# A graph layer on one core: the one-hot matrices built a pair ahead, and the gather ring released by TensorE

## The chip, the cores and the metric

The kernel runs on one core of a Trainium2 chip. Its time is the device time of one execution in microseconds (us); the timed runs give a median, and one further execution was recorded by the hardware profiler. Engines are named as the profile names them: PE is the matrix engine (PEld its weight loads), DVE the vector engine, ACT the scalar engine, POOL the general engine that also issues gathers, SP the engine that issues plain DMAs.

## What is computed

A graph of 12,500 nodes with 256 features and 212,500 directed edges (100,000 pairs both ways, and one loop per node), sorted by destination. Three parts are added up:

```python
def gcn_conv(x, W, b, src, dst, num_nodes):
    h = x @ W
    ...                                   # loops added once more, degrees, norm = dinv[s] * dinv[d]
    msg = h[s] * norm[:, None]
    out = jax.ops.segment_sum(msg, d, num_segments=num_nodes)
    return out + b

xn = _layernorm(x)
x = x + gnn(xn) + mix(xn)                 # gnn: gcn_conv(256->128), relu, gcn_conv(128->256)
x = x + ffn(_layernorm(x))                # ffn on the half of the nodes with the largest routing weight
```

`mix` is a linear attention: a softmax of the keys over all nodes, its product with the values, a normalization, and the product with the queries. `ffn` is two products (256 to 1024 to 256) with a GELU between, scaled by the node's routing weight. The segment sum over the edges, done once per layer of the GNN, is what this change is about.

## The kernel before, in words

Nodes are held in 98 tiles of 128 (`TILES`). Edges are cut into chunks of 128, sixteen chunks make a pair of batches (`PAIR`), and there are 104 pairs (`PAIRS`), 8 chunks to each batch, called a half (`HALF`). For each layer and each pair:

1. POOL (`gather_layer`, L493) issues 16 indirect gathers; each fetches 128 rows of 128 numbers from a table in DRAM (`table`) into the ring, which holds two pairs, that is four quarters of 8 chunks. Ahead of each half it waits until that quarter of the ring is free.
2. DVE builds for each half the one-hot matrices `S`: for each chunk a 128x128 matrix that says which edge goes to which node of a window of 128 nodes. It first takes each edge's distance to the start of the window (`drel`, L1162, 128x8), and then compares it with a ramp held in a PSUM bank (`ramp2`), four chunks at a time (L1171, 128x512, two per half).
3. PE (`visit`, L745) multiplies the 8 matrices with the 8 gathered chunks into PSUM bank `visit_sum[h]`, one bank for each half: 8 products, which the trace shows as 16 records (the operands are float32).
4. DVE (`add`, L1182) adds the bank into the accumulator `acc`, which lies in SBUF for all tiles; a window straddles two tiles, so there are two masked operations of 128x128.
5. DVE then releases the quarter: L1192 and L1193 in `other_visits` raise the semaphore `ring_half_free` on which POOL waits in front of the half that is two pairs later.

Where a batch reaches over more than one window of 128 nodes, further visits follow in a loop (`other_visits`).

The engines are otherwise filled with other work, written out by hand into the pairs. In layer 1, pairs 0 to 97 also take one tile each of the mixer: DVE `mix_1` (L1215 to L1221, the running maximum of the keys), ACT (L584 to L590, the exponentials), PE (L774 transposes, L780 products), DVE `mix_3` (L1226 to L1231), and PE and ACT for the next keys (L760, L767, L579, L582). DVE `finish_layer_1` (L1202, L1204) finishes a tile of the accumulator once no later edge reaches it, and SP writes it to the table of layer 2. In layer 2, pairs take the tiles' feed-forward: DVE `ff_1` (L1317, L1320), PE (L850 to L859), DVE `ff_norm` (L1326 to L1332), PE L866, ACT L612, PE L873 (first product), ACT L616 (GELU), PE L883 (second product), DVE `ff_3` (L1349, L1351) and `ff_route` (L1338 to L1343). Which tile is due in which pair stands in a control table of four words a pair (`ctl`), made during setup, that DVE and PE read into registers at the start of each pair (L329).

Order on DVE within a pair, before: read of the control words, next indices, both builds (in layer 2 with `ff_route` and `ff_1` between them), add of half 0 and its release, mixer or feed-forward work, add of half 1 and its release.

## Time and profile before

| | us |
|---|---|
| timed runs, median of 3 | 5739.89 (5737.28 to 5745.67) |
| profiled execution | 5720.82 |
| its span, first to last instruction | 5719.0 |
| setup, until POOL's first gather of layer 1 | 230.5 |
| gathers of layer 1 | 2509.4 (230.5 to 2739.9) |
| pause between the layers | 21.7 |
| gathers of layer 2 | 2806.7 (2761.6 to 5568.3) |
| last adds, feed-forward tail, selection, output | 150.7 |
| busy in the span: PE, POOL, DVE, ACT | 2936.6, 3250.5, 1904.3, 1214.9 |

An engine's busy time leaves out its register, branch and semaphore instructions. A bracket at the end of a timeline row gives the idle time of the engine before that row and what ended it: "DVEq L1193" is the release instruction in DVE's queue, "issue" that nothing the profile shows was waited for, and "remote" that the releaser could not be matched with an instruction of this core that had just ended.

### The profile page before, as it was taken

To read this page: it belongs to the slowest core of one execution; us is meant where nothing else is said; L and a number is where in the kernel's file an instruction comes from. 1 tells how busy PE (TensorE), PEld (TensorE's weight loads), DVE (VectorE), ACT (ScalarE), POOL (GpSimd) and SP (SyncE) were. 2 spreads that over 40 slices of the span, in tenths; PEclk is the share of its full clock that TensorE was granted. 3 is DMA by queue.
4 is the path that set the end of the run, shared out by engine and by line. 5 is a ranking of instruction groups with operands and counts; after the bars stand their busy time and mean duration, and the time that the engine had idled before them with its cause. 6 is when DMAs were issued, how large, how long until landed. Compare 5 with 4: busy or idle time off the path is not lost.

```text
span 5719.0 us, 69449 instructions
## 1 busy us (share of the span) xinstructions
PE 2936.6 (51%) x16356; PEld 2523.6 (44%) x16357; DVE 1904.3 (33%) x5571; ACT 1214.9 (21%) x2622; POOL 3250.5 (57%) x3443
## 2 busy tenths in 40 slices
PE   6544334444433343443266566656656666666663
PEld 5433333333333333333255455555555555555552
DVE  8433333333333233332133233323333332333336
ACT  3311111111111111110022222222223222322221
POOL 4566666666666666666555555555555555555550
PEclk8766666666666666666587778777778787787776
DMA  3211111111111111111211111111111111111115
GB/s 108 70 45 46 46 46 47 46 46 46 45 46 46 45 46 46 46 46 46 55 45 44 42 43 45 43 42 42 45 45 42 44 45 41 43 44 45 42 42 183
DMA packets 191338, 288.38 MB, mean 50 GB/s; under 512 B 59596, under 2 KB 137588, under 8 KB 191094
## 3 DMA queue, kind: packets, MB, share of 16 engines
q0 software_dynamic: 106496, 218.32, 13.4%
q1 hardware_dynamic: 83572, 68.55, 3.8%
q10 hardware_dynamic: 1232, 1.05, 0.1%
q8 instruction: 19, 0.31, 0.0%
q14 instruction: 19, 0.16, 0.0%
HBM read 249.19 MB, written 38.49 MB: 50 GB/s over the span
## 4 chain that ended last, share of the span: by engine, by line
another core or an unknown queue 34%; issue 19%; PE 16%; DVE 14%; DVEq 11%; ACT 5%; POOL 0%; DMA 0%; ACTq 0%; SPq 0%; POOLq 0%
PE bank L883 6%; PE bank L745 3%; DVEq L329 3%; PE bank L873 3%; DVE arena L1171 2%; DVE acc L1182 2%; ACT arena L616 1%; DVE drel L1162 1%; DVEq L1240 1%; DVEq L1229 1%; DVEq L1162 1%; DVE arena L1027 1%; PE bank L859 1%; DVE arena L1231 1%
## 5 line engine op out<-in xcount | busy, mean ns | idle before, releaser
L493 POOL DMA_INDIRECT arena<-table,idx_now x3328 | 3148.3, 946 | 2202.5 <-DVEq L1193 1110.8
L745 PE MATMUL bank<-arena 128*128 128x128 f32 x6656 | 1108.9, 328 | 625.3 <-issue 397.3
L745 PEld LDWEIGHTS bank<-arena 128*128 128x128 f32 x6656 | 1050.3, 242 | 667.4 <-issue 654.2
L1182 DVE SCALAR_TENSOR_TENSOR acc<-bank,from_base,acc 128x128 f32 x416 | 145.0, 349 | 1601.4 <-remote 1551.7
L774 PE MATMUL bank<-ident,arena 128*128 128x128 f32 x196 | 67.3, 447 | 1145.7 <-ACT arena L586 1130.1
L873 PE MATMUL bank<-arena 128*128 128x128 f32 x3136 | 509.5, 338 | 253.9 <-ACT arena L612 163.1
L1171 DVE TENSOR_TENSOR arena<-bank,drel 128x512 f32<-128x512 f32 x832 | 536.0, 686 | 244.7 <-issue 190.6
L873 PEld LDWEIGHTS bank<-arena 128*128 128x128 f32 x3136 | 490.8, 251 | 277.6 <-ACT arena L612 176.7
L883 PE MATMUL bank<-arena 128*128 128x256 f32 x1568 | 498.9, 479 | 159.6 <-ACT arena L616 109.3
L774 PEld LDWEIGHTS bank<-ident,arena 128*128 128x128 f32 x196 | 28.2, 203 | 1164.5 <-ACT arena L586 1148.6
L883 PEld LDWEIGHTS bank<-arena 128*128 128x128 f32 x1568 | 375.6, 248 | 261.3 <-ACT arena L616 130.4
L616 ACT ACTIVATE arena<-bank,fb1col 128x128 f32<-128x128 f32 x784 | 218.4, 374 | 1121.4 <-remote 990.5
L584 ACT ACTIVATE sm<-sm 128x2 f32<-128x2 f32 x98 | 19.9, 203 | 1653.0 <-DVEq L1222 1644.4
L780 PE MATMUL bank<-arena 128*128 128x256 f32 x392 | 203.2, 674 | 61.1 <-ACT arena L590 60.0
L1196 DVE CAST idx_now<-src_idx (+1 forms) x208 | 38.2, 184 | 510.3 <-issue 510.3
L1162 DVE TENSOR_SCALAR drel<-dst_of,tile_base,iota_n 128x8 f32 (+1 forms) x416 | 133.4, 321 | 210.4 <-issue 178.0
L760 PE MATMUL bank<-ident,arena 128*128 128x128 f32 x196 | 67.6, 449 | 218.1 <-issue 216.0
L579 ACT ACT_TABLE_LOAD x97 | 124.5, 1283 | 232.2 <-issue 165.5
L780 PEld LDWEIGHTS bank<-arena 128*128 128x128 f32 x392 | 115.0, 323 | 117.8 <-ACT arena L590 98.4
L608 ACT ACTIVATE arena<-bank 128x384 f32<-128x384 f32 x98 | 48.0, 490 | 523.5 <-PE bank L852 387.3
L760 PEld LDWEIGHTS bank<-ident,arena 128*128 128x128 f32 x196 | 28.5, 204 | 288.1 <-issue 285.3
L1182 DVE SCALAR_TENSOR_TENSOR acc<-bank,below_base,acc 128x128 f32 x416 | 142.2, 342 | 0.0
(237 smaller groups left out, 3079.6 us busy)
## 6 DMA issues: line engine op xcount, KB each, us to landing
arena<-table,idx_now POOLq DMA_INDIRECT x3328
base_rows<-arena SPq DMA_DIRECT2D x98, 128.0 KB
xs<-in_x_dram SPq DMA_DIRECT2D x6, 1792.0 KB, 16.4
acc<-base_rows SPq DMA_DIRECT2D x9, 896.0 KB, 9.8
out_dram<-acc SPq DMA_DIRECT2D x8, 896.0 KB, 7.7
table<-acc SPq DMA_DIRECT2D x7, 896.0 KB, 4.8
table<-acc SPq DMA_DIRECT2D x98, 64.0 KB
arena<-base_rows SPq DMA_DIRECT2D x5, 896.0 KB, 11.8
```

The source lines that it names most:

```text
L329: _, words = nc.values_load_multi_w_load_instructions(ctl[0:1, ds(g, 1), 0:4].rearrange("p a c -> p (a c)"), engines=[engine_type], min_val=0,
L493: pool.indirect_dma_start(ring[:, quarter * HALF + k, :], None, table[layer], bass.IndirectOffsetOnAxis(ap=idx_now[:, i, c:c + 1], axis=0) ...
L579: act.activation(xn, xs[:, ds(t, 1), :].rearrange("p a d -> p (a d)"), ACT.Identity, bias=nmr[:, ds(t, 1)], scale=rstd[:, ds(t, 1)]).then_ ...
L616: last = act.activation(H[:, k, :], pH[half][:, (k % 4) * P:(k % 4 + 1) * P], ACT.Gelu_apprx_tanh, bias=fb1col[:, k:k + 1])
L745: last = nc.tensor.matmul(visit_sum[h][:, 0:F], S[:, h, k, :], ring[:, quarter * HALF + k, :], start=(k == 0), stop=(k == HALF - 1))
L760: last = nc.tensor.transpose(pT[:, k * P:(k + 1) * P], xn[:, k * P:(k + 1) * P], ident[:, :])
L780: last = nc.tensor.matmul(pG[:, k * D:(k + 1) * D], En[:, k, :], xn, start=True, stop=True)
L873: last = nc.tensor.matmul(pH[h // 4][:, (h % 4) * P:(h % 4 + 1) * P], fw1[:, k, h * P:(h + 1) * P], T3[:, k, :], start=(k == 0), stop=(k = ...
L883: last = nc.tensor.matmul(pY[:, 0:D], H[:, h, :], fw2[:, h, :], start=(h == 0), stop=(h == KH - 1))
L1162: dve.tensor_scalar(drel[:, h, :], dst_of[:, ds(g * PAIR + h * HALF, HALF)], tile_base[:, ds(t, 1)], iota_n[:, ds(turn, 1)], ALU.subtract, ...
L1171: dve.tensor_tensor(S[:, h, 4 * q:4 * q + 4, :], bc(ramp2[:, ds(turn, P)].rearrange("p (a n) -> p a n", a=1), [P, 4, P]), bc(drel[:, h, 4 ...
L1182: last = dve.scalar_tensor_tensor(a, visit_sum[h][:, 0:F], mask[:, ds(turn, 1)], a, ALU.mult, ALU.add)
```

## The change

Four things are changed.

- The one-hot matrices of a half are built in one operation of 128x1024 that subtracts the window's start and compares at once. The starts stand in a new tile `base_col` (one column a half), which setup makes with one more PE product. `drel`, `tile_base` and their semaphores go.
- They are built a pair ahead: behind the add of half h of pair g, DVE builds half h of pair g+1. The first pair's are built ahead of each layer's loop (`first_builds`), and the last pair is written out behind the loops.
- POOL waits for PE's own signal `visit_summed` of the half two pairs earlier (it starts at 2, so that the first two pairs find the ring free). DVE no longer releases anything. PE no longer waits for the add, since DVE's build comes behind it, and it waits once per half for `S` and not twice.
- Batches that reach over several windows get a loop of their own at the start of a pair (`extra_visits`), behind which `S` is zeroed and the normal visit follows. The control words are packed anew: DVE reads three and PE two.

```diff
-            dve.sem_inc(s_free[layer], 4)
+            dve.sem_inc(s_sum[layer][h], 2)            # for each h
...
-                            pool.wait_ge(s_free[layer], gg * (2 * SETS) + (2 * i + h + 1))
+                            pool.wait_ge(s_sum[layer][h], gg * SETS + (i + 1))
...
-            def visit(layer, batch, gg, quarter, i):
-                pe.wait_ge(s_gath[layer][quarter], gg * (16 * HALF) + 16 * HALF)
-                pe.wait_ge(s_fl[layer][h], v + 1)
+            def visit(layer, gg1, g1, quarter):
+                h = quarter % 2
+                pe.wait_ge(s_gath[layer][quarter], gg1)
+                pe.wait_ge(s_S[layer][h], g1)
+                sum_half(h, quarter).then_inc(s_sum[layer][h], 1)
...
-            def build(layer, batch, g, h, i):
-                dve.tensor_scalar(drel[:, h, :], dst_of[:, ds(g * PAIR + h * HALF, HALF)], tile_base[:, ds(t, 1)],
-                                  iota_n[:, ds(turn, 1)], ALU.subtract, ALU.add).then_inc(s_drel[layer][h], 1)
-                dve.wait_ge(s_drel[layer][h], v + 1)
-                for q in range(2):
...
-                    dve.tensor_tensor(S[:, h, 4 * q:4 * q + 4, :],
-                                      bc(ramp2[:, ds(turn, P)].rearrange("p (a n) -> p a n", a=1), [P, 4, P]),
-                                      bc(drel[:, h, 4 * q:4 * q + 4].rearrange("p (c a) -> p c a", a=1), [P, 4, P]),
-                                      ALU.is_equal).then_inc(s_S[layer][h][q], 1)
+            def build(g, h, turn, base):
+                return dve.scalar_tensor_tensor(
+                    S[:, h], bc(dst_of[:, ds(g * PAIR + h * HALF, HALF)].rearrange("p (c a) -> p c a", a=1), [P, HALF, P]),
+                    base, bc(ramp2[:, ds(turn, P)].rearrange("p (a n) -> p a n", a=1), [P, HALF, P]),
+                    ALU.subtract, ALU.is_equal)
+            def build_main(layer, g, h, turn):
+                build(g, h, turn, base_col[:, ds(g * 2 + h, 1)]).then_inc(s_S[layer][h], 1)
...
+            def add_main(layer, h, place, g3):
+                dve.wait_ge(s_sum[layer][h], g3)
+                add(h, *place).then_inc(s_fl[layer][h], 1)
...
-                next_indices(0, g)
-                build(0, b0, g, 0, 0)
-                build(0, b1, g, 1, 0)
+                dve.wait_ge(s_fl[0][1], g)
+                next_indices(0, g)
+                extra_visits(0, g, at_places, extra)
                 with dve.If(f0 > 0):
                     finish_layer_1(t0)
                 if before is not None:
                     mix_3(before)
-                add(0, b0, 0, 0)
-                other_visits(0, b0, g, 0)
+                add_main(0, 0, at_places[0], g3)
+                if not last:
+                    build_main(0, g1, 0, turns[0])
                 if n is not None:
                     mix_1(g, n)
-                add(0, b1, 1, 0)
-                other_visits(0, b1, g, 1)
+                dve.wait_ge(s_fl[0][0], g1)
+                add_main(0, 1, at_places[1], g3)
+                if not last:
+                    build_main(0, g1, 1, turns[1])
...
                 next_indices(1, g)
-                build(1, b0, g, 0, 0)
+                extra_visits(1, g, at_places, extra)
                 with dve.If(f1 > 0):
                     ff_route(t1, Chain(Chain.PER - 2))
                 with dve.If(f0 > 0):
                     ff_1(t0, ch)
-                build(1, b1, g, 1, 0)
-                add(1, b0, 0, 0)
-                other_visits(1, b0, g, 0)
+                add_main(1, 0, at_places[0], g3)
+                if not last:
+                    build_main(1, g1, 0, turns[0])
                 with dve.If(f1 > 0):
                     ff_3(t1)
                 with dve.If(f0 > 0):
                     ff_norm(t0, ch)
-                add(1, b1, 1, 0)
-                other_visits(1, b1, g, 1)
+                dve.wait_ge(s_fl[1][0], g1)
+                add_main(1, 1, at_places[1], g3)
+                if not last:
+                    build_main(1, g1, 1, turns[1])
```

The order on POOL in layer 2's loop, before. One row is one instruction, `x7` seven like the one above it, and a bracket names the semaphores that a row waits for (`ring_half_free1` is raised by DVE behind the add, `visit_summed1_0` by PE at the end of a visit of half 0):

```order
L488 REGISTER_ALU [waits indices_ready1]
L493 DMA arena<-table,idx_now 128x128 [waits ring_half_free1]
L493 DMA arena<-table,idx_now 128x128 x7
L488 REGISTER_ALU
L493 DMA arena<-table,idx_now 128x128 [waits ring_half_free1]
```

And now:

```order
L482 REGISTER_ALU
L491 DMA arena<-table,idx_now 128x128 [waits indices_ready1,visit_summed1_0]
L491 DMA arena<-table,idx_now 128x128 x7
L491 DMA arena<-table,idx_now 128x128 [waits visit_summed1_1]
L491 DMA arena<-table,idx_now 128x128 x7
```

The sixteen gathers stand as they stood; what they wait for has moved from DVE to PE.

The order on DVE in layer 1's loop, from the end of `mix_3` to the start of `mix_1`, before. Ahead of these rows both builds of the same pair have been done; `visit_summed0_0` is PE's signal, and the If of `other_visits` and the release (L1192) follow the two adds:

```order
L1231 SCALAR_TENSOR_TENSOR arena<-arena,sm,bank5 128x256
L1182 ISA [waits visit_summed0_0]
L1182 SCALAR_TENSOR_TENSOR acc<-bank0,from_base,acc 128x128
L1182 ISA
L1182 SCALAR_TENSOR_TENSOR acc<-bank0,below_base,acc 128x128
L1187 REGISTER_ALU
L1187 COMPARE_AND_BRANCH
...
L1192 ISA
L1215 TENSOR_REDUCE sm<-bank3 128x2 [waits visits_added0_0,mix_keys_ready]
```

And now, up to the second build of the next pair:

```order
L1179 SCALAR_TENSOR_TENSOR acc<-bank0,from_base,acc 128x128
L1179 ISA
L1179 SCALAR_TENSOR_TENSOR acc<-bank0,below_base,acc 128x128
L1168 REGISTER_ALU x2
L1168 ISA
L1168 SCALAR_TENSOR_TENSOR arena<-dst_of,base_col,bank7 128x1024
L1234 TENSOR_REDUCE sm<-bank3 128x2 [waits mix_keys_ready]
...
L1179 SCALAR_TENSOR_TENSOR acc<-bank1,below_base,acc 128x128
L1168 REGISTER_ALU x2
L1168 ISA
L1168 SCALAR_TENSOR_TENSOR arena<-dst_of,base_col,bank7 128x1024
```

Between the add and `mix_1` the release is gone, and the first build of the next pair has come in.

## Rows read from the trace of the kernel before

**Rows 1.** Windows of both layers: length, then PE, PEld, DVE, ACT, POOL busy; PEclk.

```profile
230.50:2739.90 2509.40, 1000.10 (x4892) 845.47 (x4892) 757.98 (x2324) 351.62 (x888) 1571.57 (x1664) 0.64 0.16 46
2761.60:5568.30 2806.70, 1722.59 (x8863) 1491.93 (x8864) 867.16 (x2453) 741.07 (x1415) 1576.69 (x1664) 0.78 0.15 44
```

**Rows 2.** Waits of POOL, layer 1, 430 to 2650 us.

```profile
engine line waited for: us in total, times, longest us
POOL arena L493 <- issue: 419.4, 1376, 0.3
POOL arena L493 <- DVEq L1193: 415.2, 92, 6.5
```

**Rows 3.** The same of layer 2, 2860 to 5460 us.

```profile
POOL arena L493 <- DVEq L1193: 621.8, 111, 9.5
POOL arena L493 <- issue: 525.2, 1424, 8.5
```

**Rows 4.** Timeline, layer 1: start, duration (us), engine, operation, idle time before.

```profile
1509.70 0.94 POOL L493 DMA_INDIRECT arena<-table,idx_now  x1 [4.54 <-DVEq L1193]
...
1516.26 1.29 DVE L1171 TENSOR_TENSOR arena<-bank,drel 128x512 f32<-128x512 f32 x2
...
1517.13 3.67 PE L745 MATMUL bank<-arena 128*128 128x128 f32 x16
...
1517.50 0.35 DVE L1202 SCALAR_TENSOR_TENSOR acc<-acc,dinv,b1row 128x128 f32 x1
...
1518.44 0.94 POOL L493 DMA_INDIRECT arena<-table,idx_now  x1 [0.30 <-issue]
...
1528.43 0.94 POOL L493 DMA_INDIRECT arena<-table,idx_now  x1 [0.30 <-issue]
1532.43 0.35 DVE L1182 SCALAR_TENSOR_TENSOR acc<-bank,from_base,acc 128x128 f32 x1 [12.62 <-remote]
1532.70 0.34 DVE L1182 SCALAR_TENSOR_TENSOR acc<-bank,below_base,acc 128x128 f32 x1
...
1533.90 0.94 POOL L493 DMA_INDIRECT arena<-table,idx_now  x1 [4.53 <-DVEq L1193]
```

**Rows 5.** Timeline, end of layer 1, where no gather runs.

```profile
2748.00 6.28 PE L745 MATMUL bank<-arena 128*128 128x128 f32 x32 [16.69 <-DVE arena L1171]
...
2751.93 0.35 DVE L1182 SCALAR_TENSOR_TENSOR acc<-bank,from_base,acc 128x128 f32 x1 [1.87 <-PE bank L745]
```

**Rows 6.** Timeline, start of layer 2, behind forty gathers in a row.

```profile
2810.28 0.94 POOL L493 DMA_INDIRECT arena<-table,idx_now  x1 [0.30 <-issue]
2817.86 0.35 DVE L1182 SCALAR_TENSOR_TENSOR acc<-bank,from_base,acc 128x128 f32 x1 [33.02 <-remote]
...
2819.62 0.94 POOL L493 DMA_INDIRECT arena<-table,idx_now  x1 [8.40 <-issue]
```

**Rows 7.** Timeline, one pair of layer 2.

```profile
3625.03 0.94 POOL L493 DMA_INDIRECT arena<-table,idx_now  x1 [1.14 <-issue]
3625.56 0.38 ACT L612 ACTIVATE arena<-bank 128x256 f32<-128x256 f32 x1 [5.81 <-remote]
...
3636.87 1.61 PE L745 MATMUL bank<-arena 128*128 128x128 f32 x8 [1.83 <-issue]
...
3640.48 0.34 DVE L1182 SCALAR_TENSOR_TENSOR acc<-bank,from_base,acc 128x128 f32 x1
...
3641.95 0.94 POOL L493 DMA_INDIRECT arena<-table,idx_now  x1 [7.24 <-DVEq L1193]
```

**Rows 8.** Groups by line, layer 2: busy us, mean ns, idle before and releasers.

```profile
L745 PE MATMUL bank<-arena 128*128 128x128 f32 x3060 | 481.6, 306 | 416.6 <-issue 330.3 <-DVE arena L1171 85.3
```

**Rows 9.** Page part 5 and groups of layer 1: operations nearest to a build.

```profile
L1171 DVE TENSOR_TENSOR arena<-bank,drel 128x512 f32<-128x512 f32 x832 | 536.0, 686 | 244.7 <-issue 190.6
...
L1162 DVE TENSOR_SCALAR drel<-dst_of,tile_base,iota_n 128x8 f32 (+1 forms) x416 | 133.4, 321 | 210.4 <-issue 178.0
...
L1231 DVE SCALAR_TENSOR_TENSOR arena<-arena,sm,bank 128x256 f32<-128x256 f32 x184 | 80.2, 477 | 30.5 <-issue 25.2 <-PE bank L780 2.7
```

More of the change, by code:

```diff
@@ new lines, in control_words, with places, next_turns @@
+                ctl[0:1, ds(g, 1), first:first + n].rearrange("p a c -> p (a c)"), engines=[engine_type], min_val=0,
+                max_val=(1 << 31) - 1, skip_runtime_bounds_check_because=own_table)
+            return words
+        def places(eng, word):
+            return [(within(eng, (word >> (16 * h + 7)) & (P - 1), 0, TILES - 1),
+                     within(eng, (word >> (16 * h)) & (P - 1), 0, P - 1)) for h in range(2)]
+        def next_turns(eng, word):
+            return [within(eng, (word >> (16 + 8 * h)) & (P - 1), 0, P - 1) for h in range(2)]
@@ L990, in _ @@
             dve.memset(ones_row, 1.0)
+            dve.tensor_scalar(rrow[:, 12, :], lo_r, float(1 - P), None, ALU.add)
             link(dve.memset(zeros_b, 0.0))
@@ L1182, in add @@
                     last = dve.scalar_tensor_tensor(a, visit_sum[h][:, 0:F], mask[:, ds(turn, 1)], a, ALU.mult, ALU.add)
-                last.then_inc(s_fl[layer][h], 1)
-            def other_visits(layer, batch, g, h):
-                _, _, windows, first = batch
-                with dve.If(windows > 1):
-                    with dve.Fori(1, windows) as i:
-                        build(layer, batch, g, h, i)
-                        add(layer, batch, h, i)
-                dve.wait_ge(s_fl[layer][h], first + windows + 1)
-                dve.sem_inc(s_free[layer], 1)
+                return last
@@ new lines, in add_main, with extra_visits @@
+            def add_main(layer, h, place, g3):
+                dve.wait_ge(s_sum[layer][h], g3)
+                add(h, *place).then_inc(s_fl[layer][h], 1)
+            def extra_visits(layer, g, at_places, word):
+                with dve.If(word > 0):
+                    for h, (begin, windows) in enumerate(extra_steps(dve, mybir.EngineType.DVE, g, word)):
+                        tile, turn = at_places[h]
+                        base = sm[:, 61:62]
+                        dve.tensor_copy(base, base_col[:, ds(g * 2 + h, 1)]).then_inc(s_xb[layer], 1)
+                        dve.wait_ge(s_xb[layer], begin + 1)
+                        dve.sem_inc(s_passed, 1)
+                        with dve.Fori(0, windows) as i:
+                            build(g, h, turn, base).then_inc(s_xS[layer], 1)
+                            dve.wait_ge(s_xsum[layer], begin + i + 1)
+                            here = nc.s_assert_within(
+                                tile + i, 0, TILES - 1,
+                                skip_runtime_bounds_check_because="a window begins at or below a node of the graph")
+                            add(h, here, turn).then_inc(s_xfl[layer], 1)
+                            dve.wait_ge(s_xfl[layer], begin + i + 1)
+                            dve.tensor_scalar(base, base, float(P), None, ALU.add).then_inc(s_xb[layer], 1)
+                            dve.wait_ge(s_xb[layer], begin + i + 2)
+                            dve.sem_inc(s_passed, 1)
+                        dve.memset(S[:, h], 0.0).then_inc(s_xS[layer], 1)
+                        dve.sem_inc(s_xfl[layer], 1)
@@ L1195, in next_indices, with first_builds @@
+            def first_builds(layer):
+                now, = control_words(mybir.EngineType.DVE, 0, 0, 1)
+                for h, (_, turn) in enumerate(places(dve, now)):
+                    build_main(layer, 0, h, turn)
             def next_indices(layer, g):
@@ L1355, in ff_route_and_3, with pair_of_layer_2 @@
                 ff_3(t)
-            with dve.Fori(0, PAIRS) as g:
-                (b0, b1), (t0, f0), (t1, f1) = read_control(dve, mybir.EngineType.DVE, g)
+            def pair_of_layer_2(g, last=False):
+                g1, g3 = (g + 1, g + 3) if isinstance(g, int) else (dve.snap(g + 1), dve.snap(g + 3))
+                now, flags, extra = control_words(mybir.EngineType.DVE, g, 0, 3)
+                at_places, turns = places(dve, now), next_turns(dve, flags)
+                (t0, f0), (t1, f1) = (stage(dve, flags, k) for k in range(2))
                 ch = Chain()
+                if not isinstance(g, int) or g > 0:
+                    dve.wait_ge(s_fl[1][1], g)
                 next_indices(1, g)
-                build(1, b0, g, 0, 0)
+                extra_visits(1, g, at_places, extra)
                 with dve.If(f1 > 0):
```

210 lines of the change are left out of this document (107 added, 103 removed).

## The prediction

> **What bounds the kernel now.** I read the windows first. Both layers have the same 1,664 gathers and nearly the same POOL time (1571.57 and 1576.69 us), yet take 2509.40 and 2806.70 us [rows 1]. No engine is busy all the time in either: PE is busy 1000 of 2509 us and 1723 of 2807, DVE 758 and 867. So a chain of waits sets the time, and POOL, whose gathers start everything, is the place to read it. Per pair that is 24.1 us in layer 1 (2509.40 / 104) and 27.0 in layer 2 (2806.70 / 104).
>
> The waits of POOL come second. In layer 1 there is the regular pause of 0.30 us between two gathers (419.4 us, 1376 times), and a wait for the DVE instruction that frees a half of the ring: 92 times, 415.2 us, so 4.51 us each, once a pair [rows 2]. In layer 2 the waits sum to 621.8 + 525.2 = 1147.0 us, of which 0.30 x 1535 = 461 us are regular; about 686 us over 96 pairs, 7.1 us a pair, are stalls [rows 3]. The gathers themselves cost 16 x (0.94 + 0.30) = 19.9 us a pair: the floor under both layers.
>
> The timeline, third, shows what a stall is made of. In layer 1 POOL gathers from 1509.70 to 1529.37 (16 gathers, last start 1528.43). PE's visit 0 begins at 1517.13 and is over at 1520.80, visit 1 follows. DVE has nothing else to do from then on, and waits 12.62 us, until 1532.43, to add the visit's sum; POOL goes on at 1533.90 [rows 4]. So the sum was there 11.6 us before DVE learned of it, and DVE learned of it 3.06 us after the last gather. Where no gather runs, the same add follows PE by 1.87 us [rows 5]; behind forty gathers it waits 33.02 us, until 6.6 us after the last one (2810.28 + 0.94 to 2817.86), and POOL pauses 8.40 us [rows 6]. I read this so: what PE signals late in a long stretch of gathers is delivered only when the stretch has ended. The wait is for a signal and not for arithmetic. The Trainium skill (Perfetto Trace Analysis, section Per-instruction lifecycle) says that a matmul's reported end is an estimate and that the propagation of a semaphore is in no reported time. By that alone the 11.6 us could be a late end of PE and would stay whoever waits; but the 1.87 us of the undisturbed add holds both hidden parts, so the sum is the same by either.
>
> **The release of the ring (POOL waits for PE itself).** Before: signal of PE, two masked adds on DVE, two branch instructions, the release, POOL. Now: signal of PE, POOL. The adds take from 1532.43 to 1533.04, and POOL starts 0.86 us behind them [rows 4]. Lower bound of the gain: the adds alone, 0.61 us. Upper: POOL starts when DVE now wakes, 1.47 us. POOL needs a time of its own to answer a signal, as it needs now within the 0.86; I take 0.85 us, nearer the lower bound. The 3.06 us of late signal stay, because now it is POOL that waits for that signal. Layer 1: 102 stalls (two pairs are free at the start) x 0.85 = 87 us (62 to 150); its pause would go from 4.5 to about 3.7 us. The second half's signal has come by then, and its 0.6 us are hidden under the first half's gathers.
>
> In layer 2 DVE has work in front of the add: at 3636.87 PE runs the last eight records of a visit until 3638.48, but DVE adds at 3640.48, behind ff_1 and the second build, and POOL starts at 3641.95 [rows 7]. With the answer time of the undisturbed case (1.87 us [rows 5]) POOL could start at 3640.35, 1.6 us earlier; with 0.9 us behind PE's last record, 2.6. The second half has a pause of 1.14 us (start 3625.03), of which the add's 0.6 can go [rows 7]. Together 2.2 to 3.2 us a pair on POOL's side. I do not believe all of it: PE goes through the pair in one order, visit, ff_1, visit, ff_hidden, and its chain through ACT has delayed signals too (the copy at 3625.56 waited 5.81 us) [rows 7]. If that chain sets the period, an earlier gather only waits longer to be used. Bounds: 0.8 us (what layer 1 gains, the chain absorbs the rest) and 3.4 us (the stalls of 7.1 shrink to layer 1's new 3.7). I take 1.6 us, between 0.8 and the 2.2 that POOL's side offers at its cautious end: 102 x 1.6 = 163 us (82 to 347).
>
> **The build in one operation, a pair ahead.** Four tensor_tensor of 0.686 us and two small ones for the differences, 0.32 us each (3.4 us a pair), become two operations of 128x1024. That form is not in the trace. The nearest rows are 0.477 us for 128x256 and 0.686 for 128x512 [rows 9]; carried on by the same slope (0.209 us per 256) that is 1.10, with the slope of 1 ns an element 1.20, and two builds as they stand cost 1.37. I take 1.2, so DVE is busy 1.0 us less a pair, at most 1.2. On the path this is worth nothing in layer 1: DVE is idle for 12.62 us a pair [rows 4]. It adds one thing there: the first build now stands between the add and mix_1, so mix_1 and PE's transposes, which stand ahead of visit 0, start up to 1.2 us later. Visit 0 ended 8.6 us before the gathers did (1520.80 against 1529.37) [rows 4], so the gathers hide it. If that cover were gone it would cost 102 x 1.2 = 122 us.
> In layer 2 it takes the second build (1.3 us) from in front of the add, which is counted above, and PE no longer waits for a build (85.3 us in all, 41 times) [rows 8]. Part of that is on the chain PE to ACT to PE; it is inside my 1.6.
>
> **Port contention.** Gathers keep their 0.30 us pauses beside a build (1516.26) and beside an operation with two inputs in SBUF (1517.50 against the gather at 1518.44) [rows 4], so a long DVE operation costs POOL nothing. The Trainium skill (SBUF — State Buffer, section SBUF: two separate sides) says that GpSimd cannot write descriptors while VectorE holds the shared port pair for a whole instruction, in a two-port mode. No run here shows such a block. By the rule the new operation, int16 from SBUF against PSUM, would have to be in such a mode to hurt; that is the first slower rival below.
>
> **Control words, setup, boundary.** DVE reads three words and PE two instead of four with checks; both reads are off the path in layer 1, and I count nothing. Setup grows by some ten small linked operations; at the 0.32 us of the small L1162 [rows 9] that is +3 us. At the end of layer 1 PE's last two visits wait for their builds (16.69 us idle, then the product at 2748.00) [rows 5]; built a pair ahead, they need not. The two builds and two small operations of a half are 1.7 us, the read ahead of them about as much again: -4 us, bounds -1.7 and -6. The loop for wider batches does not run with these inputs: the 3060 records of L745 in some 96 pairs are 32 a pair, 16 for each half, no visit more [rows 8].
>
> **Sum.** -87 - 163 + 3 - 4 = -251 us of the profiled execution's 5720.82 (span 5719.0). The median of the timed runs, 5739.89, stands 19 us above it, and the difference is taken from that: 5739.89 - 251 = 5489 us, 4.4% less.
>
> **Rivals.**
> 1. The feed-forward chain sets layer 2, and only the signal path counts: 0 to 0.8 us a pair in layer 2, 0.6 in layer 1. 5740 - 61 - 41 = 5638 us. For it: PE is busiest there and ACT's waits are long. Against it: PE works 1723 of 2807 us, not all of them.
> 2. The stalls of layer 2 fall to layer 1's: 3.4 us a pair. 5740 - 87 - 347 = 5306 us. For it: both layers have the same gathers. Against it: the slow issue on PE late in the stretch of gathers (records 1.83 us apart) [rows 7].
> 3. The signals are no longer late, since POOL itself now waits for them or since the gathers fall into shorter stretches: the floor, 208 x 19.9 = 4150 us in place of 5316, less a fill: about 4600 to 4800 us. Nothing in the trace speaks for it; the lateness is there at the end of every stretch.
> 4. Slower: restarting POOL straight at PE's signal begins the next stretch of gathers before DVE, ACT and PE have taken their own signals from the one before. In layer 2, work that now slips through in the open 7 us (visit, add, GELU, the next product) then falls into the stretch, where a signal costs up to 12.6 us [rows 4] or 33 [rows 6]. It decides when visit 0's end is pushed behind the last gather by more than today's 3.8 us (3638.48 against 3641.95 - 7.24 = 3634.71) [rows 7] plus the gain. With the 8.40 us pause of rows 6 at each pair in place of 7.1, +1.3 us, and the loss of my gain, layer 2 is 130 us longer and layer 1 87 shorter: 5783 us.
> 5. Slower: a build blocks POOL for its length: 2 x 1.2 us x 208 = +500 us, less 251: about 5990. Chance 2 in 100, since no operation beside the gathers does so now.
>
> **Chances.** Forecast, with its own range of 5380 to 5600: 0.50. Rival 1: 0.20. Rival 2: 0.14. Rival 3: 0.03. Rival 4 and its weaker forms around no change: 0.11. Rival 5: 0.02. A measurement tells 0.2%, 11.5 us, from no change. Faster 0.86, same 0.03, slower 0.11. The range of 8 in 10 takes in rivals 1 and 2: 5260 to 5660 us.
>
> **What the new profile would show.** Right: POOL's stall has PE as its releaser, and is 3.5 to 3.9 us once a pair in layer 1; DVE's add in layer 1 still waits about 11 us for a late signal; one operation of 128x1024 of about 1.2 us, 416 of them; layer 2 near 25.4 us a pair. Wrong: a stall of layer 1 that stays at 4.5 us or grows (the signal comes later when POOL is the one that waits), visit 0 ending behind the last gather in layer 1, pauses between two gathers of more than 0.30 us beside a build, or a period of layer 2 at or above 27 us with PE's records spread further apart.

## The result and the profile after

The changed kernel takes 5439.59 us (median of 4 runs, 5438.04 to 5449.98), the kernel before 5738.59 (5703.95 to 5745.67). The ratio is 0.949 (95% interval 0.946 to 0.952), a gain of 299 us where 251 were forecast. The profiled execution took 5439.44 us, its span is 5437.7.

By stage, read from POOL's first and last gather of each layer in the two traces:

| us | before | after | difference | forecast |
|---|---|---|---|---|
| setup, to the first gather | 230.5 | 241.4 | +10.9 | +3 |
| gathers of layer 1 | 2509.4 | 2470.2 | -39.2 | -87 |
| between the layers | 21.7 | 15.8 | -5.9 | -4 |
| gathers of layer 2 | 2806.7 | 2564.7 | -242.0 | -163 |
| tail | 150.7 | 145.6 | -5.1 | 0 |

The rows add up to -281, the difference of the two profiled executions; the profiled one of before ran 18 us under its median.

The page after, part 5:

```profile
L491 POOL DMA_INDIRECT arena<-table,idx_now x3328 | 3144.1, 945 | 1919.3 <-issue 1338.9
...
L1168 DVE SCALAR_TENSOR_TENSOR arena<-dst_of,base_col,bank 128x1024 f32 (+1 forms) x416 | 532.3, 1280 | 19.9 <-issue 18.0
```

And POOL's row on the page before:

```profile
L493 POOL DMA_INDIRECT arena<-table,idx_now x3328 | 3148.3, 946 | 2202.5 <-DVEq L1193 1110.8
```

The build is there as one operation, 416 times, at 1.28 us (the estimate was 1.2, from [rows 9]). POOL's idle time has fallen from 2202.5 to 1919.3 us.

The windows of both layers (length, then PE, PEld, DVE, ACT and POOL busy, PE's clock), against [rows 1]:

```profile
241.40:2711.60 2470.20, 996.58 (x4908) 836.47 (x4908) 695.86 (x1913) 351.70 (x888) 1570.05 (x1664) 0.64 0.18 47
2727.50:5292.10 2564.60, 1634.87 (x8877) 1407.57 (x8877) 810.42 (x2044) 743.23 (x1419) 1573.97 (x1664) 0.81 0.18 48
```

POOL's busy time is the same as before to within 3 us; all of the gain is idle time of POOL. PE is busy 88 us less in layer 2, at a higher clock (0.81 against 0.78).

POOL's waits in mid layer 1 and mid layer 2 (us in total, times, longest), against [rows 2, 3]:

```profile
POOL arena L491 <- issue: 619.5, 1387, 4.7
POOL arena L491 <- remote: 172.2, 46, 3.8
POOL arena L491 <- PE bank L735: 17.7, 58, 0.3
POOL arena L491 <- DVE idx_now L1215: 3.6, 2, 3.3
...
POOL arena L491 <- issue: 564.7, 1393, 5.9
POOL arena L491 <- PE bank L735: 178.7, 45, 6.0
POOL arena L491 <- remote: 165.0, 68, 2.7
```

The release by DVE is gone; the one row of DVE is the wait for the next indices. In layer 1 "issue" now hides half of the stalls: its longest is 4.7 us, where an ordinary pause is 0.30. Stalls and pauses together were 835 us in the same window before, and are 813 now; in layer 2 they were 1147 in 2600 us, and are 910 in 2340.

A stretch of layer 1 (start, duration, engine, line, idle time before), against [rows 4]. The first row is the end of a visit, whose sum DVE adds at 1512.87:

```profile
1499.82 1.39 PE L735 MATMUL bank<-arena 128*128 128x128 f32 x11
...
1506.32 0.17 DVE L1240 COPY sm<-sm 128x2 f32<-128x2 f32 x1
1506.57 0.20 ACT L582 ACTIVATE sm<-sm 128x2 f32<-128x2 f32 x1 [11.87 <-DVEq L1241]
...
1507.28 0.20 ACT L584 ACTIVATION_READ_ACCUMULATOR arena<-bank,sm 128x1 f32 x1
1507.53 0.69 PE L774 MATMUL bank<-ident,arena 128*128 128x128 f32 x2 [6.32 <-ACT arena L584]
1508.45 0.94 POOL L491 DMA_INDIRECT arena<-table,idx_now  x1 [0.30 <-issue]
1512.36 0.38 ACT L588 ACTIVATE arena<-bank 128x256 f32<-128x256 f32 x1 [4.89 <-remote]
...
1512.87 0.35 DVE L1179 SCALAR_TENSOR_TENSOR acc<-bank,from_base,acc 128x128 f32 x1 [6.39 <-remote]
...
1513.95 0.94 POOL L491 DMA_INDIRECT arena<-table,idx_now  x1 [4.55 <-issue]
...
1517.48 3.75 PE L735 MATMUL bank<-arena 128*128 128x128 f32 x16
...
1521.70 0.35 DVE L1179 SCALAR_TENSOR_TENSOR acc<-bank,from_base,acc 128x128 f32 x1 [4.34 <-issue]
...
1532.67 0.94 POOL L491 DMA_INDIRECT arena<-table,idx_now  x1 [0.30 <-issue]
1536.58 0.38 ACT L588 ACTIVATE arena<-bank 128x256 f32<-128x256 f32 x1 [7.68 <-remote]
...
1537.09 0.35 DVE L1179 SCALAR_TENSOR_TENSOR acc<-bank,from_base,acc 128x128 f32 x1 [9.17 <-remote]
1537.31 0.94 POOL L491 DMA_INDIRECT arena<-table,idx_now  x1 [3.69 <-remote]
```

The stall is still there: the last gather starts at 1508.45, ends at 1509.39, and only at 1512.36 do ACT and then DVE (1512.87) go on, behind work of PE whose records end at 1508.22 and 1501.21. In the same stretch of gathers signals from DVE to ACT (1506.49 to 1506.57) and from ACT to PE (1507.48 to 1507.53) come at once: it is PE's signals that are late. The recorded semaphore updates of layer 1 say the same, in both kernels: those of DVE, ACT and POOL stand 0.01 us behind the end of their instruction, those of PE a median of 9.7 us behind it before and 3.4 us now, at most 12.1 and 13.7. The end of a PE record is modelled, so the traces leave open whether PE itself ends late or its signal is held.

What is new is where the stall stands. Before, POOL paused ahead of the first half of nearly every pair of layer 1 (3 of its 103 long pauses stood ahead of a second half). Now the first half's signal comes through in the middle of the stretch (PE's visit ends at 1521.2, DVE adds at 1521.70), and the pause is ahead of the second half. And the pauses alternate: POOL goes on 1.59 us behind ACT's wake at 1513.95, but 0.73 us behind it at 1537.31 (from 1536.58). The longer one is always ahead of the second half of an odd pair.

In layer 2, against [rows 7]:

```profile
3610.33 0.35 DVE L1179 SCALAR_TENSOR_TENSOR acc<-bank,from_base,acc 128x128 f32 x1 [8.42 <-remote]
...
3610.69 0.94 POOL L491 DMA_INDIRECT arena<-table,idx_now  x1 [2.53 <-remote]
...
3646.18 0.94 POOL L491 DMA_INDIRECT arena<-table,idx_now  x1 [5.85 <-issue]
```

POOL starts 0.36 us behind DVE's first add; before it started 1.47 us behind it (3640.48 to 3641.95). The third row is the long pause of the next pair, ahead of its second half: layer 2 still has stalls ahead of both halves.

### The profile page after: what moved, and what is told of

The parts are those of the page before. It is cut to its first block, busy times and chain, and to the rows that moved or that the text cites. A ratio compares the mean times of both kernels' runs of the same rounds, so it can differ in the third digit from the quotient of the medians.

```text
span 5437.7 us, 61242 instructions
## 1 busy us (share of the span) xinstructions
PE 2844.7 (52%) x16358; PEld 2429.4 (45%) x16359; DVE 1781.9 (33%) x4751; ACT 1216.2 (22%) x2622; POOL 3246.4 (60%) x3442
## 4 chain that ended last, share of the span: by engine, by line
another core or an unknown queue 29%; issue 28%; PE 22%; ACT 8%; DVE 7%; DVEq 3%; POOL 2%; DMA 0%; ACTq 0%; SPq 0%; POOLq 0%
PE bank L735 5%; PE bank L883 5%; PE bank L873 4%; PE bank L780 3%; DVE arena L1168 1%; ACT arena L614 1%; POOL arena L491 1%; ACT arena L584 1%; ACT L577 1%; ACT L608 1%; PE bank L760 1%; PE bank L859 1%; PE bank L663 1%; ACT arena L588 1%
## 5 line engine op out<-in xcount | busy, mean ns | idle before, releaser
L491 POOL DMA_INDIRECT arena<-table,idx_now x3328 | 3144.1, 945 | 1919.3 <-issue 1338.9
L735 PE MATMUL bank<-arena 128*128 128x128 f32 x6656 | 1082.6, 321 | 427.8 <-issue 321.5
L735 PEld LDWEIGHTS bank<-arena 128*128 128x128 f32 x6656 | 1016.2, 235 | 479.5 <-issue 404.3
L873 PE MATMUL bank<-arena 128*128 128x128 f32 x3136 | 484.6, 327 | 228.8 <-ACT arena L610 174.1
L873 PEld LDWEIGHTS bank<-arena 128*128 128x128 f32 x3136 | 466.0, 240 | 252.9 <-ACT arena L610 189.7
L883 PE MATMUL bank<-arena 128*128 128x256 f32 x1568 | 475.7, 461 | 171.9 <-ACT arena L614 115.8
L1168 DVE SCALAR_TENSOR_TENSOR arena<-dst_of,base_col,bank 128x1024 f32 (+1 forms) x416 | 532.3, 1280 | 19.9 <-issue 18.0
L780 PE MATMUL bank<-arena 128*128 128x256 f32 x392 | 203.3, 674 | 549.0 <-ACT arena L588 549.0
L883 PEld LDWEIGHTS bank<-arena 128*128 128x128 f32 x1568 | 353.2, 234 | 262.3 <-ACT arena L614 141.9
L780 PEld LDWEIGHTS bank<-arena 128*128 128x128 f32 x392 | 115.2, 324 | 604.9 <-ACT arena L588 587.3
L582 ACT ACTIVATE sm<-sm 128x2 f32<-128x2 f32 x98 | 19.9, 203 | 1141.3 <-issue 608.7
L1234 DVE TENSOR_REDUCE sm<-bank 128x2 f32<-128x256 f32 x98 | 41.5, 423 | 451.0 <-remote 360.8
L588 ACT ACTIVATE arena<-bank 128x256 f32<-128x256 f32 x98 | 37.5, 383 | 577.6 <-remote 577.6
```

The costliest lines, as they stand in the source:

```text
L491: pool.indirect_dma_start(ring[:, quarter * HALF + k, :], None, table[layer], bass.IndirectOffsetOnAxis(ap=idx_now[:, i, c:c + 1], axis=0) ...
L588: act.activation(En.rearrange("p k n -> p (k n)"), pE[:, 0:D], ACT.Copy).then_inc(s_mEe, 1)
L735: last = nc.tensor.matmul(visit_sum[h][:, 0:F], S[:, h, k, :], ring[:, quarter * HALF + k, :], start=(k == 0), stop=(k == HALF - 1))
L780: last = nc.tensor.matmul(pG[:, k * D:(k + 1) * D], En[:, k, :], xn, start=True, stop=True)
L873: last = nc.tensor.matmul(pH[h // 4][:, (h % 4) * P:(h % 4 + 1) * P], fw1[:, k, h * P:(h + 1) * P], T3[:, k, :], start=(k == 0), stop=(k = ...
L883: last = nc.tensor.matmul(pY[:, 0:D], H[:, h, :], fw2[:, h, :], start=(h == 0), stop=(h == KH - 1))
```

## The experiments

Theory A says that the signal's way from PE to POOL is the gain. Theory B says that building ahead is. Each set of kernels ran together with the kernel before, and each ratio is to that.

### First set: what part of the change gains

**Only the release moved** (`e1`, on the kernel before):

```diff
-                            pool.wait_ge(s_free[layer], gg * (2 * SETS) + (2 * i + h + 1))
+                            pool.wait_ge(s_sum[layer][h], gg * SETS + (i + 1))
...
-                dve.wait_ge(s_sum[layer][h], v + 1)
+                dve.wait_ge(s_sum[layer][h], v + 3)      # the count starts at 2
```

> The kernel before, with only POOL's wait moved from DVE's release to PE's signal; builds in three operations and in their old place. Theory A (the signal path is what gains): layer 1 loses 0.4 to 0.85 us a pair, layer 2 about 1.6, so 5738.6 - 40 to 87 - 163 = about 5490 to 5540 us. Theory B (the building a pair ahead is what gains in layer 2, since PE and the feed-forward chain set it): only layer 1 and a little of layer 2 gain, about 5650 us, and layer 2 stays above 26.5 us a pair.

Measured: 5432.70 us, ratio 0.947 (0.944 to 0.951): the whole gain of the change. Layer 1 takes 2425.3 us (-84), layer 2 2593.6 (-213). Two rows of its layer 1, the last gather ahead of a stall and the first behind it:

```profile
1515.88 0.94 POOL L493 DMA_INDIRECT arena<-table,idx_now  x1 [0.30 <-issue]
...
1520.50 0.94 POOL L493 DMA_INDIRECT arena<-table,idx_now  x1 [3.68 <-remote]
```

The pause is 3.68 us, against 4.53 before [rows 4]: 0.85 us less, as forecast. Theory A is right, B fell. The stall stays ahead of the first half here, as before.

**The builds back at their pair** (`e2`, on the changed kernel):

```diff
                 next_indices(0, g)
                 extra_visits(0, g, at_places, extra)
+                for h in range(2):
+                    build_main(0, g, h, at_places[h][1])
...
-                if not last:
-                    build_main(0, g1, 0, turns[0])
...
                     ff_1(t0, ch)
+                build_main(1, g, 1, at_places[1][1])
                 add_main(1, 0, at_places[0], g3)
```

> The changed kernel with both builds (one operation each) back at their place before: at the start of their own pair, in layer 2 one before the router step and one before the add. Theory A: POOL no longer hangs on DVE, so the place of the builds matters little: 5440 to 5480 us. Theory B: layer 2 goes back by one to two us a pair: 5550 to 5650 us.

Measured: 5446.96 us, ratio 0.950 (0.947 to 0.953), the same as the changed kernel within the intervals. Layers: 2479.3 and 2569.8 us, 9 and 5 us more than with the builds ahead. Building ahead is worth nothing that this measurement can tell, once POOL doesn't hang on DVE. The stall of layer 1 stands ahead of the second half as in the changed kernel, so it is not the place of the builds that moved it.

**The release back on DVE** (`e3`, on the changed kernel):

```diff
-                            pool.wait_ge(s_sum[layer][h], gg * SETS + (i + 1))
+                            pool.wait_ge(s_free[layer], gg * (2 * SETS) + (2 * i + h + 1))
...
                 add(h, *place).then_inc(s_fl[layer][h], 1)
+                dve.wait_ge(s_fl[layer][h], g3 - 2)
+                dve.sem_inc(s_free[layer], 1)
```

> The changed kernel, but POOL again waits for a release that DVE gives behind its add (and ahead of the next build). Theory A: 0.8 us a pair more in layer 1 (about 85 us) and 0.8 to 1.6 in layer 2 (80 to 160): 5600 to 5680 us. Theory B: half of it or less, since DVE now reaches its add without a build in front: 5480 to 5520 us.

Measured: 5673.11 us, ratio 0.990 (0.987 to 0.993). Layer 1 takes 2593.1 us, 84 more than before the change; layer 2 takes 2670.1, 137 less. From its layer 1:

```profile
1514.01 0.94 POOL L492 DMA_INDIRECT arena<-table,idx_now  x1 [0.30 <-issue]
...
1518.47 0.35 DVE L1181 SCALAR_TENSOR_TENSOR acc<-bank,from_base,acc 128x128 f32 x1 [9.76 <-remote]
...
1520.80 0.94 POOL L492 DMA_INDIRECT arena<-table,idx_now  x1 [5.84 <-issue]
```

POOL goes on 2.33 us behind the start of DVE's add (this is the half with the longer answer; before it was 1.47). Against the changed kernel, layer 1 takes 123 us more, where 85 were expected. So everything in the change but the release is worth 1%: it loses 84 us in layer 1, where the stall stands ahead of the second half here too, and gains 137 in layer 2. That the latter comes of the add no longer standing behind a build is read from the order on DVE, not tested by itself. With the release on PE the same thing is worth nothing, since POOL doesn't ask for the add: the two gains are not to be added up.

**mix_1 ahead of the build** (`e4`, on the changed kernel):

```diff
+                if n is not None:
+                    mix_1(g, n)
                 if not last:
                     build_main(0, g1, 0, turns[0])
-                if n is not None:
-                    mix_1(g, n)
```

> The changed kernel with the first build of the next pair behind mix_1 in layer 1, and not ahead of it. If the gathers hide mix_1 (as predicted), no change: 5430 to 5450 us. If the mixer's chain is late by the build's 1.28 us and sets when the second half's signal goes out, layer 1 gains up to 1.2 us a pair: 5320 to 5400 us.

Measured: 5442.32 us, ratio 0.949 (0.946 to 0.952); layer 1 2469.6 us against 2470.2. The build's 1.28 us in front of the mixer is hidden, as forecast. Here too the stall stands ahead of the second half. What moved it there is left among the rest of the change (control words, the order of waits on PE, the build in one operation), which no run takes apart.

### Second set: what makes the signals late, and a set in which none was

**Two gathers of eight** (`e6`), **the ring turned** (`e7`), **a pause behind each fourth gather in layer 1** (`e8`), **no loop for wide batches** (`e9`), all on the changed kernel:

```diff
-                            for k in range(HALF):                       # e6
+                            for k in range(2):
...
-                                    ring[:, quarter * HALF + k, :], None, table[layer],          # e7
+                                    ring[:, place_of[quarter] * HALF + k, :], None, table[layer],   # [3, 0, 1, 2]
...
                                 ).then_inc(s_gath[layer][quarter], 16)      # e8
+                                if k % 4 == 3 and layer in (0,):
+                                    idled[0] += 1
+                                    pool.memset(arena[:, 11400:11400 + 512], 0.0).then_inc(s_idle[layer], 1)
+                                    pool.wait_ge(s_idle[layer], gg * 16 + idled[0])
...
-                extra_visits(0, g, at_places, extra)      # e9, on DVE and PE, both layers
```

> The changed kernel with two gathers in each half and not eight; PE multiplies the eight matrices with these two chunks in turn (six of eight gathers are left out, all products stay). Theory A (PE's signals are held back by long stretches of gathers): a pair's gathers are over in 5 us, no signal is late, DVE's add follows PE by about 1.9 us, and a pair of layer 1 takes 12 to 16 us, one of layer 2 16 to 20. Theory C (PE's products end late by themselves, or their signal takes 9 to 12 us whatever POOL does): the add still waits 9 us or more behind PE's last record, and a pair of layer 1 stays above 20 us.

> The changed kernel with the ring's quarters laid to other addresses (first half of even pairs into the last quarter, the others one further down); order, semaphores and code stay. In the changed kernel POOL starts its first gather 0.77 us behind the end of a wait, but 1.62 us where the gather goes to the last quarter (second half of odd pairs). If that goes with the address, the second halves of odd pairs start 0.85 us earlier: about 45 us less in layer 1 (where nearly all pauses are ahead of second halves) and 0 to 20 in layer 2, 5375 to 5400 us. If it goes with the place in the code or the semaphore: no change, 5440 us.

> The changed kernel; in layer 1 POOL clears a spare 128x512 piece of SBUF behind every fourth gather and waits for the end of it (an idle DMA queue of about 1 us, four times a pair). Theory A with short memory (a stretch under 5 us delays no signal and a short pause ends it): DVE's adds follow PE in 2 us, the 4 us pause of a pair vanishes and four of about 1 us take its place: layer 1 within 1% of now, pause about 4 us in all, 5400 to 5480 us. Theory A with long memory (a pause of 1 us doesn't let the signals through): the stall stays and the pauses come on top, 3 to 4 us a pair, 5750 to 5850 us.

> The changed kernel without the loop for batches over several windows (code and branch are left out; no batch of these inputs needs it). If the loop costs nothing but its branch: no change, 5430 to 5445 us. If the longer code or the branch costs 0.2 us a pair on the path of the signals: 20 to 40 us less.

The kernel before took 4544.20 us in this set (19 runs, 4538.73 to 4551.30) where it had taken 5732.50 in the first. `e7` took 4547.10 us (ratio 1.001, 1.000 to 1.002), `e9` 4546.54 (1.000, 1.000 to 1.001), `e8` 5075.92 (1.116, 1.115 to 1.118), and `e6` 3153.48 (one run; it leaves out six gathers of eight). The changed kernel itself did not run in this set; `e7` and `e9` are its nearest variants. POOL's waits in layer 1 of `e9` (430 to 2200 us), and a visit with its add:

```profile
POOL arena L491 <- issue: 432.1, 1418, 0.3
...
1512.67 3.59 PE L735 MATMUL bank<-arena 128*128 128x128 f32 x16 [5.56 <-DMA arena<-table,idx_now]
...
1516.85 0.35 DVE L1177 SCALAR_TENSOR_TENSOR acc<-bank,from_base,acc 128x128 f32 x1 [7.04 <-PE bank L735]
```

No pause of POOL is longer than 0.3 us. The add follows PE's last record (1512.67 + 3.59 = 1516.26) by 0.59 us, in the middle of a stretch of gathers that never ends, and its releaser is read as PE and not as "remote". In the kernel before, at the same place of the program, the add came 11.6 us behind PE's last record [rows 4]. PE's recorded updates, too, now stand 0.01 us behind their records. A pair takes 19.97 to 19.99 us in both layers of `e7` and `e9` (median from one first gather to the next), close to POOL's own 16 x (0.94 + 0.30) = 19.8. So the late signals are no property of the program: the kernel before took 5732 us in the first set and 4544 in this one, on the same chip. Where they are absent the change is worth nothing (`e7` and `e9` against before: 1.001 and 1.000), because POOL's gathers are the bound. What sets the condition, no run here shows. The traces differ in one more thing: of the 16 semaphore updates with which each gather reports, that of `e9` holds over 99%, that of the kernel before 15 to 26%. Whether this is part of the cause or of the recording isn't shown. The questions of `e7` and `e9` were not answered in layer 1's stall, since there was none; that the wide loop costs nothing is shown for this condition only.

`e6` still says something, since its gathers are short:

```profile
805.12 0.94 POOL L491 DMA_INDIRECT arena<-table,idx_now  x1 [0.30 <-issue]
...
809.73 3.73 PE L735 MATMUL bank<-arena 128*128 128x128 f32 x16
...
813.93 0.35 DVE L1179 SCALAR_TENSOR_TENSOR acc<-bank,from_base,acc 128x128 f32 x1 [4.84 <-PE bank L735]
...
814.27 0.94 POOL L491 DMA_INDIRECT arena<-table,idx_now  x1 [8.20 <-PE bank L735]
```

The add follows PE's last record (813.46) by 0.47 us, where 1.9 were expected, and POOL waits for PE. With a quarter of the gathers a pair takes 12.8 us in layer 1 and 14.7 in layer 2 (16 to 20 were expected): that is what all other work needs per pair while no signal is late, far under POOL's 19.97. Of theory C the part "whatever POOL does" fell by this and by `e9`. But nothing was late in this set, so `e6` does not show that shorter stretches cured it, and neither run can tell whether in the late condition PE ends late or its signal is held. In layer 2 of the kernel before it is not the signal alone, as the row ahead of PE's in [rows 7] shows:

```profile
3634.77 0.27 PE L745 MATMUL bank<-arena 128*128 128x128 f32 x1 [1.83 <-issue]
```

The next product of the same visit starts at 3636.87, 2.1 us later, and PE waits for nothing that the profile shows. In that layer 210 products start 0.6 to 3 us behind the one before them in their visit; in `e7` and `e9` none does.

### Third set: the same questions with late signals

> The changed kernel once more, as it is. In the second set of experiments the kernel before took 4544 us in place of 5739, and no signal was late; this run shows under which of the two conditions the present set runs. With late signals: before about 5735, this about 5440 us, ratio 0.95. With prompt signals: POOL issues without a pause (19.97 us a pair), both take about 4544 us, ratio 1.00 within 0.2%.

Measured: 5501.78 us, before 5821.50 (7 runs), ratio 0.945 (0.941 to 0.950). Late signals were back, and the gain with them. (Both kernels took 1 to 2% longer than before.)

> The ring with turned quarters once more, since its question can only be answered where POOL pauses. With late signals: 5375 to 5400 us if the 0.85 us go with the address, 5440 if with the place in the code or the semaphore. With prompt signals: 4547 us again.

Measured: 5506.42 us, ratio 0.945 (0.941 to 0.950): no change. Rows of its layer 1, ACT's wake and POOL's first gather behind it, for an even and an odd pair:

```profile
1500.66 0.39 ACT L589 ACTIVATE arena<-bank 128x256 f32<-128x256 f32 x1 [8.36 <-remote]
...
1501.39 0.95 POOL L492 DMA_INDIRECT arena<-table,idx_now  x1 [3.82 <-remote]
...
1524.33 0.38 ACT L589 ACTIVATE arena<-bank 128x256 f32<-128x256 f32 x1 [2.15 <-PE bank L775]
...
1525.91 0.94 POOL L492 DMA_INDIRECT arena<-table,idx_now  x1 [4.81 <-issue]
```

POOL follows by 0.73 us and by 1.58 us, as without the turn. So the extra 0.85 us belongs to the second half of odd pairs and not to the address of the ring. Nor does it belong to the semaphore: the kernel before waits for one and the same semaphore ahead of all four halves, and from the semaphore's update to POOL's start it takes 0.80 us at three of them and 1.65 at the second half of odd pairs (one stall of layer 1, 20 of layer 2). That leaves the place in the code; no run moves it.

> A pause of about 1.3 us behind every fourth gather in layer 1, once more, one look. With late signals and short memory: the adds of layer 1 follow PE by 2 us, a pair takes about 25 us, the pauses alone (5400 to 5500 us). With late signals and long memory: the stall of 4 us comes on top, 28 to 29 us a pair, 5850 to 5950 us. With prompt signals: 25 us a pair again, 5076 us.

Measured: 5613.51 us (one run). Layer 1 takes 2602.7 us, to 0.2 us the 2602.5 of the second set, where no signal was late; layer 2, without pauses, takes 2600.2, as without the edit (2604.5 in the run above). A pause of it:

```profile
1512.45 0.94 POOL L493 DMA_INDIRECT arena<-table,idx_now  x1 [0.30 <-issue]
...
1513.39 0.54 POOL L500 MEMSET arena<- 128x512 f32 x1
...
1514.74 0.95 POOL L493 DMA_INDIRECT arena<-table,idx_now  x1 [0.81 <-issue]
```

A gap of 1.35 us behind every fourth gather (1513.39 to 1514.74) takes all late signals out of layer 1: PE's recorded updates stand 0.01 us behind their records there, at most 0.05. It costs more than it gives there (24.6 us a pair against 24.0), and the next run asks whether a shorter gap will do.

### Last run: short pauses in both layers

```diff
+                                if k % 4 == 3:
+                                    idled[0] += 1
+                                    pool.memset(sm[:, 62:63], 0.0).then_inc(s_idle[layer], 1)
+                                    pool.wait_ge(s_idle[layer], gg * 16 + idled[0])
...
```

> The changed kernel with POOL clearing one column (128x1) behind every fourth gather and waiting for it, in both layers: a pause of about 0.9 us (0.10 for the clearing, 0.81 until the next gather, as in the run before) in place of 0.30, four times a pair, so 2.4 to 3.3 us a pair on top of POOL's 19.97. With late signals and if a pause of 0.9 us is long enough to let them through: 22.6 to 23.3 us a pair in both layers, 5120 to 5250 us, ratio to before 0.88 to 0.91, faster than the changed kernel. If 0.9 us is too short: the pauses come on top of the stalls, 5700 us or more. With prompt signals (before at 4544): 5050 to 5150 us, ratio 1.12, slower than before.

Measured: 5282.35 us (6 runs), before 5727.02 (11 runs), ratio 0.922 (0.920 to 0.925). With late signals it is faster than both kernels. Against the changed one, which did not run beside it, that is 2.8% by the first ratio (0.922 / 0.949) and 2.4% by the repeat (0.922 / 0.945). It missed the expected 5250 by 32 us, all of it in layer 2 (23.8 us a pair, at most 23.3 expected). This run and its kernel before ran on another chip than the three sets, so the late signals belong to no single chip. Layer 1 takes 2421.5 us, layer 2 2470.0. From layer 1:

```profile
1503.97 3.78 PE L743 MATMUL bank<-arena 128*128 128x128 f32 x16 [2.89 <-DMA arena<-table,idx_now]
...
1508.10 0.11 POOL L500 MEMSET sm<- 128x1 f32 x1
1508.22 0.35 DVE L1187 SCALAR_TENSOR_TENSOR acc<-bank,from_base,acc 128x128 f32 x1 [6.81 <-PE bank L743]
...
1509.02 0.94 POOL L493 DMA_INDIRECT arena<-table,idx_now  x1 [0.81 <-issue]
```

A gap of 0.92 us (1508.10 to 1509.02) is enough in layer 1: PE's visit ends at 1507.75, and DVE adds at 1508.22; PE's updates are 0.01 us late in the median and over 1 us in 1 of 100. In layer 2 it is not: PE's updates are still 1.6 us late in the median and up to 13 us, and one gap in 23 is over 2.2 us, longer than any in layer 1 (18 of 415). With prompt signals this version was not run; each pair would pay the four gaps, some 3 us (22.8 against 19.97), so it would be slower than both.

## Why the prediction was right

The forecast was 5489 us, the time is 5440, and the mechanism is the one named: late signals of PE, a shorter way for them to POOL. Part of it is luck: layer 1 gave less than half of its term and layer 2 half as much again, and the two misses partly cancel. So is the condition of the chip: in the other one the gain would have been nothing.

- **Signals held back by gathers.** Right as far as the gathers go: the two runs with pauses (`r4`, `e10`) let PE's signals through in layer 1 by gaps in the stretch alone. "For a signal and not for arithmetic" is more than is shown, since PE's own end may be late (see the second set).
- **The undisturbed add, 1.87 us.** Misread. The 1.87 us of [rows 5] are DVE's idle time ahead of the add and not its distance from PE. The record of that row holds two visits and ends at 2754.28, and the second visit's add follows by 0.17 us:

```profile
2754.45 0.35 DVE L1182 SCALAR_TENSOR_TENSOR acc<-bank,from_base,acc 128x128 f32 x1 [1.90 <-PE bank L745]
```

- **Release, layer 1: 0.85 us a pair, 87 us.** Right for the edit by itself: `e1` shows 84 us and a pause of 3.68 us. In the whole change only 39 us were left. The step that failed is that the pause "would go from 4.5 to about 3.7 us" and stay ahead of the first half: it moved to the second half, and there every other one costs 0.85 us more (4.55 us and 3.69 us), 0.43 us a pair or 45 us. So the prediction's own sign of being wrong, a stall that stays at 4.5 us, came for every second pair, and its sign of being right, PE as the releaser, came in layer 2 only. The rows of before hardly showed this cost, since only 3 stalls of layer 1 stood ahead of a second half. Why the stall moved is open.
- **Layer 2: 1.6 us a pair, 163 us.** Too small: 2.3 us a pair, 242 us, in `e1` 2.0 and 213. POOL's side had offered 2.2 to 3.2. The lower end rests on the misread 1.87 us; with the 0.80 us that POOL takes behind a semaphore's update it is 2.7 + 0.6 = 3.3 us, by an estimate. Of these 2.3 came, where the deduction for the feed-forward chain had left 1.6. How much that chain does take when signals are late, no run isolates; `e6` shows only that without late signals all other work of a pair of layer 2 takes 14.7 us.
- **The build: 1.2 us, nothing on the path.** 1.28 us; `e2` and `e4` show that neither its place nor its order to the mixer tells. The 1.3 us of the second build in front of the add tell only while DVE gives the release (`e3` gains 137 us in layer 2, `e2` loses 5), so it was right to count it inside the release and not beside it.
- **Port contention.** 416 operations of 128x1024 left POOL's 0.30 us pauses as they were (`e9`: none longer). Rival 5 fell. The Trainium skill (SBUF — State Buffer, section SBUF: two separate sides) describes a block for two-port modes of VectorE; this operation, which reads int16 from SBUF and float32 from PSUM, shows none, and whether any operation of this kernel runs in such a mode no run shows.
- **Setup, boundary.** Between the layers -5.9 for -4. Setup +10.9 for +3, but it is not the code alone: `e1`, whose setup is that of before, has its first gather at 238.3 us against 230.5, so a profiled setup can't tell 8 us.
- **Rivals.** Rival 3, the floor at which no signal is late, got 3 chances in 100, "nothing in the trace speaks for it". It came, in the second set, as a condition of the chip: 4544 us for the kernel before, 4547 for two variants of the changed one. Its price of 4600 to 4800 us was too high; the sum behind it has a slip too (208 x 19.9 is 4139, not 4150). The trace of one condition couldn't show the other. Rival 4, the slower one, fell: both layers got shorter.

## What to carry to other kernels

When an engine waits far longer than its producer's last record explains, and a queue of gathers runs meanwhile, suspect a late signal. Take engines out of the signal's way before you make their work faster, and test whether a short gap in the gathers lets it through. Two edits that shorten the same wait don't add up: undo each alone. And run the kernel before beside every experiment: here its own time went from 5732 to 4544 and back to 5822 us between sets on one chip, more than any edit that kept all the work.

## What was not expected of the hardware

- The same kernel took 4544 us or 5727 to 5822 us, by whether PE's signals are late during gathers. In the slow case signals late in a stretch arrive about 3 us behind the last of 16 gathers (1509.39 to 1512.36); in the other case the add follows PE by 0.59 us.
- Of the engines only PE is late. In layer 1 of the kernel before, the recorded updates of PE come a median of 9.7 us behind their records, those of DVE, ACT and POOL 0.01 us. In layer 2 PE also starts products late (single records with gaps of 1.83 us).
- A gap of 0.92 us in the gathers, after at most four of them, ends the hold in layer 1. In layer 2 it does so only in part.
- POOL starts a gather 0.80 us behind the semaphore's update, or 1.65 us for one of its four halves, wherever the ring's data lie and whatever semaphore it waits for.
